# Softmax attention on one NeuronCore: scores from three bf16 parts on the whole array, and from two rounded 32-bit parts in two row groups

## What is computed

```python
q, k, v = proj(Wq), proj(Wk), proj(Wv)        # 16 heads of 16 columns
q = q * cos + _rotate_half(q) * sin
k = k * cos + _rotate_half(k) * sin
att = jnp.einsum('bhqd,bhkd->bhqk', q, k) / math.sqrt(hd)
att = jax.nn.softmax(att + mask, axis=-1)      # causal mask
out = jnp.einsum('bhqk,bhkd->bhqd', att, v)
return out.transpose(0, 2, 1, 3).reshape(B, T, D) @ Wo.T
```

## Time and profile before

| | |
|---|---|
| median of three runs | 1175.94 us (1169.95 to 1176.4) |
| time of the profiled execution | 1176.6 us |
| its span, first to last instruction | 1174.9 us |
| granted TensorE clock, mean | 0.988 of full speed |
| PE busy | 1110.7 us (95%) |
| PE weight loads busy | 861.1 us (73%) |
| DVE busy | 613.1 us (52%) |
| ACT busy | 618.5 us (53%) |
| POOL busy | 479.7 us (41%) |

### The profile page before, as it was taken

How to read it: one execution, slowest core, us unless ns; L and a number is a source line. 1 busy time by engine, 2 the same in 40 slices (tenths; PEclk the granted TensorE clock), 3 DMA queues, 4 the chain that set the end, 5 groups by cost and what they waited for, 6 DMA issues and landing times. The chain is left out here.

```text
span 1174.9 us, 33305 instructions
## 1 busy us (share of the span) xinstructions
PE 1110.7 (95%) x14272; PEld 861.1 (73%) x14272; DVE 613.1 (52%) x1361; ACT 618.5 (53%) x1166; POOL 479.7 (41%) x513
## 2 busy tenths in 40 slices
PE   5999999999999999999998998978899999997998
PEld 4888888888888888888887787756344444435777
DVE  5243433333343545454536644996777777733642
ACT  4544444444444555555546565534567776774662
POOL 2354454444454646555535366301122222221355
PEclk9999999999999999999999899999999999998999
DMA  3100101001010020020031200273022222000001
GB/s 126 54 2 10 46 3 46 10 2 60 2 47 15 16 74 23 29 74 23 22 129 39 82 1 1 79 204 96 14 56 56 56 55 56 2 2 1 1 19 54
DMA packets 15951, 49.58 MB, mean 42 GB/s; under 512 B 2433, under 2 KB 7105, under 8 KB 13121
## 3 DMA queue, kind: packets, MB, share of 16 engines
q1 hardware_dynamic: 15808, 47.50, 13.9%
HBM read 36.54 MB, written 10.75 MB: 40 GB/s over the span
## 5 line engine op out<-in xcount | busy, mean ns | idle before, releaser
L1658 DVE TENSOR_REDUCE aa_mx<-aa_S 128x1 f32<-128x640 f32 (+1 forms) x192 | 177.2, 955 | 53.0 <-PE aa_S L1455 49.9
L1589 ACT ACTIVATE aa_PT<-aa_ST 128x512 f32<-128x512 f32 (+1 forms) x304 | 159.0, 579 | 71.6 <-PE aa_ST L1481 68.7
L500 DVE SCALAR_TENSOR_TENSOR la_y<-la_g,la_O 128x512 f32<-128x512 f32 x64 | 41.1, 684 | 225.0 <-PE la_O L678 225.0
L590 PE MATMUL la_R<-a_hTh,WF 128*128 128x512 f32 x384 | 130.5, 405 | 4.6 <-DVE a_hTl L147 4.6
L1389 POOL TENSOR_SCALAR_AFFINE_SELECT aa_PT<-aa_PT 128x256 f32<-128x256 f32 (+1 forms) x112 | 48.5, 440 | 177.6 <-ACT aa_PT L1589 177.2
L298 POOL TENSOR_TENSOR la_yl<-la_y,la_yh 128x512 fp32r<-128x512 f32 x62 | 79.3, 1302 | 93.0 <-ACT la_yh L376 93.0
L285 POOL TENSOR_TENSOR la_qd<-q,la_C 128x512 f32<-128x512 f32 x64 | 81.0, 1285 | 80.8 <-PE la_O L678 80.5
L507 DVE TENSOR_TENSOR X<-la_R,X 128x512 f32<-128x512 f32 x64 | 44.3, 692 | 122.8 <-PE la_R L590 122.7
L1452 PE MATMUL aa_S<-aa_stacks 96*128 96x512 bf16 (+3 forms) x384 | 97.8, 330 | 10.2 <-DVE aa_mx L1658 7.1
L1481 PE MATMUL aa_ST<-aa_stacks 99*128 99x512 bf16 (+3 forms) x384 | 99.6, 328 | 3.1 <-ACT aa_PT L1589 1.6
L1000 POOL TENSOR_TENSOR f_fl<-f_f,f_fh 128x512 fp32r<-128x512 f32 x48 | 61.6, 1294 | 92.0 <-ACT f_fh L892 92.0
(11 more groups left out here) (217 smaller groups left out, 2804.2 us busy)
## 6 DMA issues: line engine op xcount, KB each, us to landing
la_Wraw<-w_quads_dram SPq DMA_DIRECT2D x7, 1280.0 KB, 6.4
aa_stacks<-k_parts SPq DMA_DIRECT2D x16, 256.0 KB, 6.7
q_parts<-aa_QP SPq DMA_DIRECT2D x4, 768.0 KB, 4.5
aa_stacks<-q_parts SPq DMA_DIRECT2D x8, 384.0 KB, 4.7
k_parts<-aa_KP SPq DMA_DIRECT2D x4, 768.0 KB, 3.8
qw_w<-w_ffn_dram SPq DMA_DIRECT2D x12, 192.0 KB, 2.4
q_ffn<-qw_w SPq DMA_DIRECT2D x12, 192.0 KB, 1.9
X<-hidden_dram SPq DMA_DIRECT2D x4, 512.0 KB, 7.6
```

Source lines behind the costliest of these rows:

```text
L590: m = pe.matmul(out, a, b, start=n == 0, stop=n == len(pairs) - 1)
L1589: act.activation(PT[:, (NM2 * g + b) % NPT, h:h + nh, 0:w], ST[at % NB][:, 0:nh * w].rearrange("p (h q) -> p h q", h=nh), ACT.Exp, scale=S ...
L1658: dve.reduce_max(out, src, AXX).then_inc(s1_free, 1)
```

## The change

Queries and keys are cut into two parts, a rounded 32-bit one (float32r) and the rest, in place of three bf16 parts. A stack then has three products of parts, 48 rows, and with the two rows of the maximum 50. The heads of a group go in twos: one in rows 0 up, the other in rows 64 up, and their products are issued as a pair, each into a bank of its own. The array then works in two row groups (tiles of 64 rows x 128 columns); masks and transposes take the whole array as before, value products the 32-column tiles. The program's counts in a steady group: 96 score products and 32 mask products before and after, 38 steps before and 20 after, with 38 and 40 exponentials. Changes between kinds of tile: 24 before, 53 after.

```diff
-NPART = 3
-SROWS = 6 * SD
+NPART = 2
+SROWS = 3 * SD
...
-Q_RUNS = ((0, 3), (0, 2), (0, 1))
-K_RUNS = ((0, 2), (0, 2), (0, 1), (2, 1))
-ND = len(Q_RUNS) + len(K_RUNS)
+HALVES = 2
+Q_RUNS = ((0, 1), (0, 2))
+K_RUNS = ((0, 2), (0, 1))
+ND = HALVES * (len(Q_RUNS) + len(K_RUNS))
...
-    q_parts, k_parts = (nc.dram_tensor(n, (BATCH, NPART, SD, SH // 2, 2, SEQ), BF16).ap()
+    q_parts, k_parts = (nc.dram_tensor(n, (BATCH, NPART, SD, SH // 2, 2, SEQ), F32).ap()
...
-        NSL, NPT, NB, RS = 3, 3, 3, 3
+        NSL, NPT, NB, RS = 3, 3, 3, 2
...
-        V = sb("V", [P, NT, SH, 32], F32)
+        V = sb("V", [P, NT, SH, SD + 1], F32)
...
-        SEGS = [(0, i, t) for i in range(2) for t in range(4)] + [(1, j, t) for j in range(HG) for t in range(4)]
+        SEGS = [(0, i, t) for i in range(2) for t in range(4)] + [(1 + f, i, t) for i in range(2) for t in range(4)
+                                                                  for f in range(2)]
...
-            nh = {4: 1, 3: 1, 2: 2, 1: 4}[span(qb, kt)[1] // P]
-            STEPS += [(b, h, nh) for h in range(0, HG, nh)]
+            STEPS += [(b, 0, 2)] if span(qb, kt)[1] <= 2 * P else [(b, 0, 1), (b, 1, 1)]
...
-        VALUES_AT = [max(LAST[b] + 3, (LAST + [NST + LAST[0]])[b + 1]) for b in range(NM2)]
+        VALUES_AT = [max(LAST[b] + 2, (LAST + [NST + LAST[0]])[b + 1]) for b in range(NM2)]
...
-                row = min(done + 9, need - 4)
-                part = min(done + 3, row - 1)
+                row = min(done + 5, need - 2)
+                part = min(done + 2, row - 1)
```

```diff
-                for j, col, k0, k1 in runs:
-                    ins = pe.matmul(bank[:, col:col + k1 - k0], Q[0:SROWS, j, qt * P:(qt + 1) * P],
-                                    K[0:SROWS, j, k0:k1], start=True, stop=True)
-                    if k1 == (qt + 1) * P:
-                        ins = pe.matmul(bank[:, col + k1 - P - k0:col + k1 - k0], MK[:, 0, :], MK[:, 1, :],
+                for m in range(HALVES):
+                    r = slice(64 * m, 64 * m + SROWS)
+                    ins = pe.matmul(bank[:, m * TB:m * TB + w], Q[r, i, qt * P:(qt + 1) * P], K[r, i, k0:k0 + w],
+                                    start=True, stop=True)
+                if kind != 1:
+                    for m in range(HALVES):
+                        ins = pe.matmul(bank[:, m * TB + w - P:m * TB + w], MK[:, 0, :], MK[:, 1, :],
                                         start=False, stop=True, skip_group_check=True)
...
-                    ins = pe.transpose(ST[at % NB][:].bitcast(BF16)[:, t * P:(t + 1) * P],
-                                       NM[:, h, t].rearrange("p j r -> p (j r)"), MK[:, 0, :])
+                    ins = pe.transpose(ST[at % NB][:, t * P:(t + 1) * P],
+                                       NM[:, h, t].rearrange("p j r -> p (j r)").bitcast(F32), ident[:])
...
-                if at >= NB:
-                    pe.wait_ge(st_free, at - NB + 1)
-                for e in range(nh):
-                    ins = pe.matmul(ST[at % NB][:, e * w:(e + 1) * w], KS[g % NSL][0:KROWS, h + e, kt * P:(kt + 1) * P],
-                                    QS[g % NSL][0:KROWS, h + e, q0:q0 + w], start=True, stop=True)
-                ins.then_inc(st_ok, 1)
+                if at >= NB - 1:
+                    pe.wait_ge(st_free, at - NB + 2)
+                for e in range(ni):
+                    for m in range(HALVES):
+                        r = slice(64 * m, 64 * m + KROWS)
+                        ins = pe.matmul(ST[(at + m) % NB][:, e * w:(e + 1) * w],
+                                        KS[g % NSL][r, i0 + e, kt * P:(kt + 1) * P], QS[g % NSL][r, i0 + e, q0:q0 + w],
+                                        start=True, stop=True)
+                        if e == ni - 1:
+                            ins.then_inc(st_ok, 1)
```

More of the change, by code:

```diff
@@ L1259, in attention @@
         LAST = [max(n for n in range(NST) if STEPS[n][0] == b) for b in range(NM2)]
-        CUT = [n for n, (b, h, nh) in enumerate(STEPS) if blocks[b][1] >= 4 * blocks[b][0] and (h + nh) % 2 == 0]
-        VALUES_AT = [max(LAST[b] + 3, (LAST + [NST + LAST[0]])[b + 1]) for b in range(NM2)]
-        step_cols = [nh * span(*blocks[b])[1] for b, h, nh in STEPS]
+        CUT = [n for n, (b, i, ni) in enumerate(STEPS) if blocks[b][1] >= 4 * blocks[b][0]]
+        VALUES_AT = [max(LAST[b] + 2, (LAST + [NST + LAST[0]])[b + 1]) for b in range(NM2)]
+        step_cols = [2 * ni * span(*blocks[b])[1] for b, i, ni in STEPS]
         GCOLS, ACOLS = sum(seg_cols), sum(seg_cols[:HALF[0]])
@@ L1301, in attention @@
                 for row in ROWS_AT.get((g, n), []):
-                    RINGT[("rows",) + row] = len(RINGT)
-                RINGT["step", g, n] = len(RINGT)
+                    RINGT[("rows",) + row] = used
+                    used += 1
+                RINGT["step", g, n] = used
+                used += 2
                 for seg in segments(g, n):
@@ L1312, in attention @@
         V_PIECES = {A_SEGS + 1 + 2 * v: v for v in range((N_AHEAD - A_SEGS) // 2)}
-        V_STEPS = {n: v for n, v in enumerate(range(len(V_PIECES), NT // 2), 1)}
+        V_STEPS = {n: v for n, v in enumerate(range(len(V_PIECES), NT // 2))}
         block = mem.enter_context(nc.Block())
@@ L1338, in _ @@
                     sp.wait_ge(l_ok, 1)
+                    ln["turned"](sp)
+                    ones(0)
                     for i in range(2):
@@ L1357, in _ @@
             load(2)
+            ones(2)
             for i in range(4):
@@ L1382, in parts @@
[L1382 to L1383 removed]
+                pool.tensor_tensor(nm(1), mr[:, h], nm(0).bitcast(F32), ALU.subtract).then_inc(nm_ok, 1)
             def cut(g, n):
[L1386 to L1389 removed]
+                b, i, ni = STEPS[n]
@@ L1390, in cut @@
+                pool.wait_ge(st_free, RINGT["step", g, n] + 2)
+                part = PT[:, (NM2 * g + b) % NPT, 2 * i:2 * (i + ni), 0:P]
+                pool.affine_select(part, part, [[0, 2 * ni], [1, P]], ALU.is_ge, 0.0, base=0,
                                    channel_multiplier=-1).then_inc(cut_ok, 1)
-            def ones(slot):
-                pool.memset(KS[slot][SROWS:KROWS, :, :].rearrange("r j t -> r (j t)").bitcast(F32),
-                            TWO_ONES).then_inc(one_ok, 1)
+            pool.tensor_scalar(ONE[:], ident[0:MROWS, :], 0.0, 1.0, ALU.mult, ALU.add).then_inc(init_ok, 1)
@@ L1490, in values @@
                 else:
-                    pe.wait_ge(st_free, RINGT["step", g, LAST[b]] + 1)
+                    pe.wait_ge(st_free, RINGT["step", g, LAST[b]] + 2)
                 if b == 0 and g == 0:
@@ L1577, in rows @@
                     act.wait_ge(row_in[h], 64 * g)
-                act.activation(MXT[:, h, :], ST[at % NB][:].bitcast(BF16)[:, 0:TB], ACT.Copy).then_inc(st_free, 1)
+                act.activation(MXT[:, h, :], ST[at % NB][:], ACT.Copy).then_inc(st_free, 1)
                 act.wait_ge(st_free, at + 1)
@@ L1676, in _ @@
             dve.wait_ge(rot.r_in, 16)
-            for n in range(NS + 2):
+            for n in range(NS + 1):
                 if n < NS:
```

187 lines of the change are left out of this document (83 added, 104 removed).

## The result

The changed kernel takes 1197.53 us (median of 4 runs, 1196.5 to 1206.35), beside 1176.17 us of the kernel before on the same chip: ratio 1.0201, 95% interval 1.0173 to 1.0229. Forecast was 1168, with a range of 1150 to 1196. Of the four executions that of 1206.35 us had a mean granted clock of 0.961, the others 0.976 to 0.979. The profiled one has a span of 1194.8 us, 19.9 more than before, and a mean granted clock of 0.979 (before 0.988).

The account below looks back on a forecast made before the run. The prediction took PE (TensorE) to bound the steady groups, and DVE the projection. Groups -1, entry -6, V pieces -1, first group and tail 0, about -8.5 on 1176.6, gave 1168 us, range 1150 to 1196.

Parts of the forecast that it names:

- Pairs overlap: Score products: a pair runs side by side, columns -7.0 us a group; rival without overlap 1216 us, chance 0.05.
- free row halves: Rival: in attention groups, leaving the row halves costs nothing, -2.0 us a group, total 1156; chance 0.23.
- Weight loads of a pair: Score pairs: two loads go side by side, 0.105 exposed at each of 21 entries, +2.2 us a group.
- content forecast -1.5: Steady group: PE's own work, columns, mode changes, loads and transposes summed, goes from 29.3 to 27.8 us.
- Projection steps: Entry: one DVE subtraction goes, PE then sets the step at 2.74 us, from 3.2 before.
- keys come: Entry: keys for the first score product expected 3 to 6 us earlier, within a term of -6.
- The serial-load rival: Score pairs: two weight loads come one after the other, +3.9 us a group, total 1195; chance 0.17.
- the score banks: Steady groups: bank loop of 1.07 us for 512 columns makes 6 of 20 steps wait, 2.0 us a group.
- The tail: After the steady groups, 1027.8 to 1068.6: 512-column block 2.47 us against 2.39, given back elsewhere, sum 0.
- Steady groups: Six groups from 842 to 1027.8: 30.7 us each against 30.93, -0.2 a group, -1 in all.
- The entry's forecast of -7: Entry, 734 to 808 us: -6 from shorter projection steps and earlier keys, -1 from five V pieces.

Follow-up runs that it names:

- e4: The changed kernel with each exponential over half its columns, the other weights set to one before the first group: 1188.02 us, ratio 1.01.
- e10: e5 with five score banks instead of three in the last group's second query half: 1177.53 us, ratio 1.0013.
- e1: The changed kernel with first-pass segments moved out of steps that hold a value block, same instructions in another order: 1196.58 us, ratio 1.0179.
- e5: e1 with the sync engine putting a group's second set of maxima into the stacks before loading the next stacks: 1186.82 us, ratio 1.0107.
- e12: e10 with three 512-column products that nobody reads added in the first group: 1176.35 us, ratio 0.9996.
- e7: e5 without the mask products of the first pass: 1177.05 us, ratio 1.0025.
- e9: e5 with products that nobody reads added in the last group's waits: 1180.33 us, ratio 1.0038.
- e3: The changed kernel with each 128-row mask product cut into two 64-row ones in the scores' row groups: 1202.26 us, ratio 1.0179.
- e6: e5 with the masks cut into 64-row parts as in e3: 1188.86 us, ratio 1.0097.

## Why the prediction was wrong

**Right.** Pairs overlap; a change between row halves and the whole array costs 0.095 to 0.11, no free row halves. Weight loads of a pair go side by side, exposed 0.12 for both (forecast 0.105). The Trainium skill, "TensorEngine Tiling (Array Packing)", Key Properties, has it that changing the tiling mode drains TensorE; the 0.095 to 0.11 above agree. The Trainium skill, "TensorE: Matmul & The Clock Gate", Weight-path perf modes, has the fast weight load only for weights that are not FP32; a load of 189 ns in the changed kernel, beside 98 for the masks' bf16 ones, fits that. PE's busy time a group fell by 1.1 us (content forecast -1.5). Projection steps take 2.72 us (2.74), keys come 5.45 earlier (3 to 6). The serial-load rival gave nearly the measured time, 1195, and 33 us as the mark of its group, and was still not the cause: a like total by another mechanism.

**The step that failed: the score banks.** "The tail shows that loop: ... 0.42 + 0.60 + 0.05 = 1.07 us for 512 columns" and "6 of 20 steps are shorter ...: 2.0 us". The 0.42 was taken from a bf16 product whose load was hidden. The new pair has its 32-bit load exposed on every entry, and also behind every wait, so it is 0.53 to 0.60 to ACT's start, and in the rows above 0.60: loop 1.25. The load is 0.11 or 0.12 of the 0.18 more; where the other 0.06 comes from no run shows. That loops of this kind would bound short steps was foreseen; the term was sized too small. In the steady groups seven steps start late behind the exponential that frees their bank, by 0.30 to 0.95 us, 4.0 us a group, where the sum had six steps and 2.0. (This is an estimate from the starts on PE: the distance to the pair, less the 0.15 that a mask or the 0.23 that a pair of 512 columns costs where nothing waits.) e4 shortens that loop by 0.21 and the tail block by 0.20; e10 removes it and the block goes to 2.0; e1 and e5 fill it by order (in e5 the same estimate gives 1.4 us a group).

Steady groups came out 14.8 us over the forecast (+13.8 for -1), 2.5 a group; 2.0 of them are that term. The other 0.5 was not taken apart: PE's busy time fell by 0.4 less than the content, and the maxima's DMA and ACT's copies add stops. Order and the maxima's queue (e5) give 2.2 us a group back, 11.9 over the six (187.18 for 199.07), and with them the period is 30.95, near the forecast 30.7.

**The tail**, forecast at 0, cost 6.9 us: 512-column blocks of 2.65 in place of 2.39 (forecast 2.47), by the same loop, and around the last turns of the query half two stops in a row (0.71 and 0.52 us, 0.74 and 0.57), with 3.4 us at half clock at each (1061.7 to 1065.1, 1072.0 to 1075.4; clock 0.93 over 47.67).

**What no rival held: the clock.** The prediction took clock 1.00 for the whole stretch. The entry's forecast of -7 became +0.65, with the clock at 0.74 from 797 to 843; that the clock is the cause there is not shown (e12 had a higher clock and no gain clear of the spread). In the steady groups the changed kernel kept full clock (longest stop 0.8), and e1 to e4 lost it in some groups. Part of the work saved on PE came back as stops, and behind some stops the clock was half. No length of stop parts them: in the groups of e1 and e4 the four stops of 1.33 to 1.67 us for the maxima were each followed by 10 to 14 us at 0.50, of the five from 0.73 to 0.99 two were and three were not, the kernel before kept full clock behind a stop of 1.15 us (1043.15), and e7 has three low stretches of 3.4 us in its groups (from 898.2, 959.7 and 990.4 on) with no stop over 0.52 in the 10 us before them.

**Left open.** Why the first group takes longer: from the first score product to the first turned output it is 60.3 us before, and 63.7 to 66.4 in the changed kernel, e5, e9 and e10, whose code is the same there; the clock stays at 0.50 for 13.7 us in it. The 7.65 us by which the entry missed are a good quarter of the 28 by which the sum did (14.8 are the steady groups, 6.9 the tail, -1.4 what comes after attention). Whether e5's move of SP's order alone, without the deal, would help was not tried.

## What to carry to other kernels

When a step takes two of three banks at once, write down the loop from product to reader to bank for the new product, its exposed load included, and lay the order of the work against it before counting columns. Once PE is no longer the bound, taking more from it may gain little (e3, e6): look at the granted clock behind each stop, and remove the longest stop first. Here the simple edit to the old layout (no masks in the first pass, 0.9948) was not beaten by any version of the new one; the best of them, also without masks, has 0.996, and the intervals overlap.

## What the runs showed that was not expected

- With 30 products more the tail was 8.1 us shorter (51.90 to 43.80), at clock 1.00 in place of 0.77.
- A 1.33 us stop was followed by 10.2 us at clock 0.50, with PE busy throughout (10.13 of 10.15 us); a stop of the same kind that was 0.32 us long (968.86 in the changed kernel) was not followed by any.
- A 32-bit weight load is exposed not only after a change of tile but after a wait: the pair at 1079.07 follows a pair of the same tile and still lasts 0.49 us, where a product in a stream lasts 0.39.
